# Attention output products over two packed groups of heads instead of four, with one more GpSimd sum per pair

## What is computed

```
# layer 0 (with a key mask); layer 1 is the same with a bias and no mask
q, k, v = x @ Wq.T, ctx @ Wk.T, ctx @ Wv.T          # 16 heads of 16
attn = softmax(scale * q_h @ k_h.T, axis=-1)        # per head h
out = concat_h(attn_h @ v_h) @ Wo.T                 # the output product
x = layernorm(x + out)
```

## Time and profile before

| | |
|---|---|
| Median of three runs | 2223.26 us (2219.47 to 2227.24) |
| The profiled execution | 2219.07 us |
| its span, first to last instruction | 2217.0 us |
| Mean granted TensorE clock | 0.925 of full speed |
| PE busy | 1857.7 us (84%) |
| DVE busy | 1084.9 us (49%) |
| ACT busy | 932.1 us (42%) |
| POOL busy | 262.7 us (12%) |
| Narrow attention, from its first q product to its last write to X | 294.9 to 579.6 us |
| Wide attention | 957.0 to 1694.6 us |

### The profile page before, as it was taken

One profiled execution on the slowest core, in us unless ns is written; L12 is line 12 of the kernel. 1 busy time (PEld: TensorE's weight loads), 2 busy tenths in 40 slices (PEclk: granted clock), 3 DMA queues, 4 the chain that ended last, 5 costly groups with the idle time before them and its releaser, 6 DMA issues.

```text
span 2217.0 us, 27165 instructions
## 1 busy us (share of the span) xinstructions
PE 1857.7 (84%) x7552; PEld 797.6 (36%) x7553; DVE 1084.9 (49%) x1481; ACT 932.1 (42%) x1663; POOL 262.7 (12%) x215
## 2 busy tenths in 40 slices
PE   6789969999799685848999999999996369999980
PEld 2334422332244232313333333333322346666650
DVE  4663258776211324439887688788741212111215
ACT  3331236677411424232777677577684012211210
POOL 4143010000200202120000000000002410000005
PEclk9999979999899797977999999999998589999995
DMA  9101051100100002280000000000003510000003
GB/s 332 34 31 46 0 118 30 30 27 11 54 0 0 5 0 25 22 144 22 8 16 9 9 16 8 9 15 8 2 1 162 215 46 24 28 28 28 26 26 111
DMA packets 64088, 95.78 MB, mean 43 GB/s; under 512 B 11504, under 2 KB 56752, under 8 KB 62074
## 3 DMA queue, kind: packets, MB, share of 16 engines
q1 hardware_dynamic: 60922, 86.21, 13.4%
q0 software_dynamic: 3072, 8.39, 1.2%
HBM read 65.20 MB, written 28.97 MB: 42 GB/s over the span
## 4 chain that ended last, share of the span: by engine, by line
PE 55%; DVE 5%; issue 5%; POOL 3%; ACT 3%; DMA 1%; SPq 0%; DVEq 0%; ACTq 0%; POOLq 0%
PE ps L517 9%; PE ps L1793 9%; PE ps L1148 8%; PE ps L1170 8%; PE ps L1107 8%; PE ps L1808 5%; DVE arena L1302 2%; PE ps L1450 2%; PE ps L1205 1%; POOL rows_in L1902 1%; PE ps L441 1%; POOL arena L1907 1%; PE ps L1801 1%; DMA qparts<-arena 1%; ACT arena L1861 1%
## 5 line engine op out<-in xcount | busy, mean ns | idle before, releaser
L1251 ACT ACTIVATE arena<-ps 128x512 f32<-128x512 f32 x1088 | 575.1, 600 | 242.9 <-PE ps L1170 241.4
L1302 DVE TENSOR_REDUCE arena<-ps 128x1 f32<-128x802 f32 (+1 forms) x512 | 480.6, 985 | 106.2 <-PE ps L1107 104.9
L517 PE MATMUL ps<-arena 128*128 (+1 forms) x832 | 383.0, 621 | 73.6 <-DVE arena L1591 23.2
L1107 PE MATMUL ps<-arena 97*128 97x401 bf16 (+2 forms) x1280 | 347.9, 354 | 47.8 <-DVE arena L1302 18.1
L1170 PE MATMUL ps<-arena 100*128 100x512 bf16 x1088 | 370.2, 385 | 10.0 <-ACT arena L1251 5.2
L1148 PE MATMUL ps<-arena 128*32 128x512 f32 x2176 | 289.8, 605 | 1.4 <-ACT arena L1251 1.4
L517 PEld LDWEIGHTS ps<-arena 128*128 128x128 f32 x832 | 164.3, 199 | 291.2 <-issue 291.2
L1793 PE MATMUL ps<-arena 128*128 x608 | 198.8, 470 | 29.3 <-ACT arena L1861 29.3
L1107 PEld LDWEIGHTS ps<-arena 97*128 97x128 bf16 x1280 | 114.1, 99 | 237.4 <-DVE arena L1302 109.3
L1170 PEld LDWEIGHTS ps<-arena 100*128 100x128 bf16 x1088 | 104.9, 98 | 260.4 <-ACT arena L1251 186.5
L1988 DVE TENSOR_TENSOR arena<-ps,arena 128x352 f32<-128x352 f32 x76 | 40.0, 526 | 269.4 <-ACT arena L1868 197.3
(11 more groups left out here) (187 smaller groups left out, 1451.4 us busy)
## 6 DMA issues: line engine op xcount, KB each, us to landing
arena<-in_experts_w SPq DMA_DIRECT2D x8, 2176.0 KB, 16.9
arena<-qparts SPq DMA_DIRECT2D x192, 64.0 KB, 2.3
qparts<-arena SPq DMA_DIRECT2D x48, 128.0 KB, 2.0
rows_in<-arena SPq DMA_DIRECT2D x1, 5120.0 KB, 35.5
arena<-in_ctxT SPq DMA_DIRECT2D x3, 1664.0 KB, 9.6
kparts<-arena SPq DMA_DIRECT2D x24, 208.0 KB, 2.4
arena<-kparts SPq DMA_DIRECT2D x12, 416.0 KB, 14.6
arena<-rows_in SPq DMA_DIRECT2D x38, 128.0 KB, 2.0
```

The lines of the kernel that those rows point to most:

```text
L517: ins = eng.matmul(out, w[:, k, m * P:(m + 1) * P], x[:, k, tok(c)], start=k == 0, stop=k == ktiles - 1)
L1107: ins = eng.matmul(slot_banks(s_static)[:, x, 0:n_keys], Qst[0:97, ring, heads[x], q * P:(q + 1) * P], Kst[0:97, at_head(ring * HG + heads ...
L1251: eng.activation(probs[:, keys_of(u, kt) % 2, h, :], ring_bank(r), ACT.Exp, bias=0.0).then_inc(ring_read.sem, 1)
L1302: eng.tensor_reduce(MX[:, par, heads[0] * QT + q, n % 2:n % 2 + 1], got, AX.XY, ALU.max).then_inc(slot_free.sem, 1)
```

## The change

- `On` has two slots instead of four. In `Vaug`, the odd groups have the keep flag in column 0 and their values in columns 16 to 31 of each strip, so that their outputs come out in rows 16 to 31. Even groups are as before.
- GpSimd multiplies an even group into `On`. For an odd group it multiplies in place in `Osb`, waits for its own result, and adds it to the slot of the even group before it: one more sum of 128 by 512 per pair.
- `out` sums over two packed pairs instead of four groups.
- `out_w` is loaded in eight transfers of half the size each instead of four, and the two unused slots stay zero.
- The denominator row must come out as zero, since the other group uses its partition. The exponential at line 1238 gets a bias per partition, `den_bias`, of -200 on that row and 0 elsewhere. DVE computes it at the start of each attention with four small instructions, from `pick_den` and a copy rotated by 16 rows, `pick_odd`, loaded by two more transfers. ACT waits for it once.
- The placing of the values (line 1266) is two activations of 128 columns per key tile instead of one of 256; the keep column is set with four copies instead of one.

```
-        On, Osb = f32(a0, HG, CH), f32(a0 + G * CH, 2, CH)
+        On, Osb = f32(a0, 2, CH), f32(a0 + G * CH, 2, CH)
...
             for j in range(HG):
-                eng.dma_start(out_w[0][32 * j:32 * j + DH, :, :],
-                              io["w_out0"][:, j, :, :].rearrange("g i n -> i g n")).then_inc(ld_xw[0], 16)
+                for r in range(2):
+                    eng.dma_start(out_w[0][32 * j + DH * r:32 * j + DH * (r + 1), 0:2, :],
+                                  io["w_out0"].rearrange("(q r) j i n -> q r j i n", r=2)[:, r, j, :, :]
+                                  .rearrange("q i n -> i q n")).then_inc(ld_xw[0], 16)
             eng.wait_ge(mask_row_done, 1)
...
                     if c == 0:
                         all_free(eng)
+                        eng.dma_start(pick_odd[0:P - DH, :], io["pick_den"][DH:P, :]).then_inc(const_rows.sem, 16)
+                        eng.dma_start(pick_odd[P - DH:P, :], io["pick_den"][0:DH, :]).then_inc(const_rows.sem, 16)
...
-                    for g in range(G):
-                        ins = eng.matmul(slot_banks(s_static)[:, 0, :], wo_w[:, g, m * P:(m + 1) * P],
-                                         On[:, g, :], start=g == 0, stop=g == G - 1)
+                    for q in range(2):
+                        ins = eng.matmul(slot_banks(s_static)[:, 0, :], wo_w[:, q, m * P:(m + 1) * P],
+                                         On[:, q, :], start=q == 0, stop=q == 1)
...
-                    eng.activation(Rden[:, (u - 1) % 2, :], Rden[:, (u - 1) % 2, :], ACT.Exp, bias=0.0,
-                                   scale=-1.0).then_inc(den_inv.sem, 1)
+                    eng.activation(Rden[:, (u - 1) % 2, :], Rden[:, (u - 1) % 2, :], ACT.Exp,
+                                   bias=den_bias[:, (u - 1) % 2:(u - 1) % 2 + 1], scale=-1.0).then_inc(den_inv.sem, 1)
...
-                    eng.activation(Vaug[:, t, :, 0:DH], ps[:, 4 + t % 4, 0:D].rearrange("p (h d) -> p h d", h=H),
-                                   ACT.Copy, scale=keep_cols[:, t:t + 1]).then_inc(v_in.sem, 1)
+                    for r in range(2):
+                        eng.activation(Vaug_pairs[:, 2 * t:2 * t + 2, r, :, DH * r:DH * (r + 1)],
+                                       ps[:, 4 + t % 4, 0:D].rearrange("p (q r j d) -> p q r j d", r=2, j=HG, d=DH)
+                                       [:, :, r, :, :], ACT.Copy, scale=keep_cols[:, t:t + 1]).then_inc(v_in.sem, 1)
...
-                    eng.tensor_tensor(On[:, (u - 1) % 4, :], Osb[:, (u - 1) % 2, :], Rden[:, (u - 1) % 2, :],
-                                      ALU.mult).then_inc(o_norm.sem, 1)
+                    g, rden = (u - 1) % 4, Rden[:, (u - 1) % 2, :]
+                    if g % 2 == 0:
+                        eng.tensor_tensor(On[:, g // 2, :], Osb[:, 0, :], rden, ALU.mult).then_inc(o_norm.sem, 1)
+                    else:
+                        eng.tensor_tensor(Osb[:, 1, :], Osb[:, 1, :], rden, ALU.mult).then_inc(o_norm.sem, 1)
+                        o_norm.wait(eng, normalised(u, c) - 1)
+                        eng.tensor_tensor(On[:, g // 2, :], On[:, g // 2, :], Osb[:, 1, :], ALU.add).then_inc(o_norm.sem, 1)
...
             @part("dve")
             def _(eng):
+                const_rows.wait(eng, 16 * 8)
+                for r, pick in enumerate((pick_den, pick_odd)):
+                    eng.tensor_reduce(den_bias[:, r:r + 1], pick, AX.X, ALU.max).then_inc(den_bias_set.sem, 1)
+                for r in range(2):
+                    den_bias_set.wait(eng, 2)
+                    eng.tensor_scalar(den_bias[:, r:r + 1], den_bias[:, r:r + 1], UNUSED_ROW, None, ALU.mult)\
+                        .then_inc(den_bias_set.sem, 1)
```

69 lines of the change are left out of this document (41 added, 28 removed).

## The result

| | before | changed |
|---|---|---|
| median of 4 runs, us | 2225.25 (2219.47 to 2227.99) | 2204.78 (2204.28 to 2205.49) |
| ratio, 95% interval | | 0.9912 (0.9890 to 0.9933) |
| profiled execution, us | 2219.07 | 2205.07 |
| its span, us | 2217.0 | 2203.2 |

The kernel became faster by 0.9%. The forecast was 2207.0 in a range of 2199 to 2215. Stage by stage the two spans differ by -13.8 us, where the sum of the prediction was -15.2. Much of the 20 us between the medians lies in the runs of before: its profiled execution was the fastest of them. A second pair of profiles, with spans of 2220.6 and 2202.9, differs by -17.7.

What follows compares the result with a forecast made beforehand. The matrix engine was taken to set the pace in both loops. Terms -20.9 - 4.3 + 5.4 + 1.6 + 2.4 + 0.6 = -15.2 us gave 2203.9 or 2208.1 by base; 2207 was taken, range 2199 to 2215.

Steps and rivals of the forecast that it cites:

- What bounds the kernel: Both attention loops: the matrix engine sets the pace; halving the output products saves 3.5 us in six blocks, -20.9 us.
- The two ends: Behind each attention's last unit: GpSimd's sum adds 1.33 us, eight fewer products save 3.5; -4.3 us for both.
- slow stretch covers more: End blocks: the low clock may cover all 8 records, 4 more at twice the pace, +1.7 us per end.
- GpSimd's sum holds DVE: Odd narrow units: DVE's two-operand product of the cut waits for GpSimd's sum, 1.0 us late; +5.4 us together.
- DVE is not held: Rival for the narrow units: the sum begins after DVE's last product has the port; 5.4 us fall away, 2201.5; chance 0.20.
- held harder: Rival: DVE's cast before the product is caught too, +1.9 us; with slow ends, 2212; joint chance 0.20.
- The mixer's start: First layer's front: four more weight load issues delay the mask row's store and DVE's first copy; +1.6 us.
- a late start stays late: First layer's mixer: DVE starts a serial chain there, so the delay of its first copy persists; +1.6 us.
- The biases: Before each attention's first reduction: four small DVE instructions cost 1.2 us while the matrix engine waits; +2.4 us.
- the loads of `pick_odd`: Two loads ahead of the q parts: 0.6 us in the wide attention's saturated transfers, nothing in the narrow.
- The wide loop's edge: In the wide unit holding the loop's edge: it costs some 2.3 us more, which the change leaves in place.
- code loading: Rival at the narrow loop's edge: shorter blocks no longer cover a gap, worst case 7 us lost, 2214; chance 0.08.

Runs made afterwards that it cites:

- added sum: The kernel before, with GpSimd also adding two normalised arrays into an unread array behind each odd product; 2227.61 us, ratio 1.0021.
- mask row first: The changed kernel with the mask row's store issued ahead of the clearing stores and the output weights' loads; 2204.65 us.

## Why the prediction was right

*What bounds the kernel.* Right. The products saved came off each block in full, 3.44 us of the 3.5 forecast, -20.6 for the six against -20.9. Putting them back cost 29.4 us.

*The two ends*, forecast -2.2 each. The narrow one gave -2.1 to -2.3, the wide one -0.9 to -1.9, about -3.7 together for -4.3. The sum and its hand-over took the 1.33 us forecast, and the pause before the block was 4.13 us. The bound "slow stretch covers more" is what the second profile's wide end shows.

*GpSimd's sum holds DVE*, +5.4. This was the step that could most easily have been wrong, and it was right in mechanism and size: the cut at 1.38 us, the next item on the matrix engine late by 0.45, 0.78 us a unit and 5.45 in all where only the sum is added. Unit 6 alone gave 0.72 where the prediction had 1.0. In the changed kernel it was 0.96 a unit and 6.1 in all (201.40 - 205.61 + 3 x 3.44); the difference holds the 0.08 us of every unit that stays open. With the sum moved behind the cut, 6.0 of it went. The rival "DVE is not held" is out. In all seven odd narrow units the cut's last instruction starts 0.03 to 0.04 us behind the sum, so only a little decided. The cast before it got through between GpSimd's two instructions, at 0.24 us, so the rival "held harder" is out in that part. The reductions from PSUM were not held: in the wide attention they run beside the sums and take 0.98 to 0.99 us there as elsewhere, and a wide turn less its edge's gap lost 3.4 us, the products alone.

*The mixer's start*, +1.6. This step failed. The eight loads took 3.62 us of issue instead of 1.77, as forecast. But the mask row's landing didn't follow: the copy came 1.26 us behind the start of that store's issue (53.62 to 54.88), where before it had come 2.2 us behind (51.97 to 54.15). The first copy started at 54.9 to 56.3 in the changed kernels against 54.2 to 55.9 before. Above all, "a late start stays late" found no support. The copy's 0.73 us were gone by 185 us, and with the copy 7 us earlier the next step waited for the matrix engine and nothing behind it came sooner. Worth 0, as far as the spread lets one see.

*The biases*, +2.4, and *the loads of `pick_odd`*, +0.6 in the wide and nothing in the narrow attention. The sum was somewhat high: 3.0 forecast, 2.0 in the narrow and 0.3 in the wide prologue measured against before by the means of six profiles, though 3.1 and 0.6 in the first. Its parts were off. From the flags' copy to the first reduction it is 1.15 us instead of 0.52, so the four instructions cost 0.63 where I took 1.2. A reduction of 128 columns took 0.24 and the small scaling 0.11. The loads seem to cost something in the narrow attention, where I had them at nothing: behind the clearing, ACT had the first q part 1.3 us later in the first profile (18.0 against 16.7 us), but not in all of them (16.1 to 18.3 over the six). What else varies there is the clock: it was back at 1.00 from 33.0 to 33.8 us behind the clearing on in the three profiles of the kernel before and its added sum, and from 33.7 to 36.8 on in the six.

*The wide loop's edge*, "which the change leaves where it is". This was wrong. The gap grew on average from 2.27 to 2.52 us (+0.5 for the two edges), and the clock fell at nearly half of them, for 1.6 to 3.2 us each. In the two profiles of the changed kernel and the one of the mask row first, turns 1 and 2 together are 1.7 us above what the products alone give. The narrow edge showed no gap at all; the rival "code loading" is out there.

Term by term the stages give -20.6 for the loops' products, -3.7 for the ends, +6.1 for the held cut, nothing for the mixer, +2.3 for the prologues and +1.7 for the edges: -14.2 for the forecast -15.2. So the sum was near partly because its misses cancel: 1.6 and 0.7 too much for the mixer and the prologues, against 1.7 too little at the edges and 1.6 for products, ends and held cut together. That is luck. That 2207 stood 2 us from the median of 2204.8 says less still: the medians of the kernel before lie between 2220.8 and 2225.3 in five comparisons, the two of the changed kernel at 2204.5 and 2204.8, and the 16 to 20 us between them aren't fully accounted for by stages. The base was a choice between 2203.9 and 2208.1.

## What to carry to other kernels

A sum that moves from the matrix engine to GpSimd is paid where VectorE reads two operands from SBUF in the same moment, here 0.8 to 1.0 us a unit; look for the small instructions on the path, and give the sum a wait that puts it behind them. At the end of a stage, put every product that can be ready ahead of the last wait. Extra ones paid here too: without a pause the clock stayed up in six ends of six. A cost at the front counts only if the next step doesn't wait for another engine.

## What the runs showed of the hardware

- DVE's product of two SBUF operands that started 0.04 us after GpSimd's sum took 1.38 us instead of 0.28, and one that started 0.10 us after took 1.31. A cast that began while GpSimd's product was ending took 0.24. The gap between GpSimd's two dependent instructions, 0.08 us (378.36 + 1.27 to 379.71), let it through.
- A small cast from SBUF to SBUF that began 0.5 to 0.6 us inside GpSimd's product took 0.75 and 0.85 us instead of 0.21. A cast and a difference that read PSUM took their usual 0.28 us under the same product, and so did reductions from PSUM under the sum (0.98 us).
- In the wide loop's edge the matrix engine stands still for 2.2 to 3.0 us with "issue" as the reason, and the narrow loop's shows no such gap.
- At such a gap the granted clock may fall to 0.50 (1.2 GHz) for 3 to 7 us. This was at 9 of 20 edges behind short blocks of products and at none of 8 behind long ones. In two profiles neither edge had it, in another both did, and the gap's length didn't decide.
- At the six ends of 12 records without a pause the clock stayed at 2.4 GHz. Of the 22 ends with a pause of 2.4 to 4.1 us before the last products, 20 had records 0.85 us apart. The two others (pauses of 2.69 and 2.40 us) ran at 0.43 throughout.
- A load issued by the SP queue took 0.44 us of issue at 64 KB and 0.45 at half of that (1.77 us for four, 3.62 for eight).
